# The first layer of a hybrid network: constants, norm and low-rank products inside one block

## What is computed

```python
h = layernorm(x)                       # 1024 rows of 256
q, k, v = (silu(conv4(h @ W, c)) for W, c in ((Wq, cq), (Wk, ck), (Wv, cv)))
w = l2norm(silu(conv4(h @ Ww, cv)))
g = log_sigmoid(h @ Wf1 @ Wf2)         # decay of each slot
beta = sigmoid(h @ Wb)                 # write strength of each head
o = gsa2_scan(q, k, v, w, g, beta)     # recurrence over 512 tokens
gate = h @ Wg1 @ Wg2 + bg2
x = x + (rms_norm(o) * norm_w * sigmoid(gate)) @ Wo
```

## Time and profile before

| | us |
|---|---|
| median of 3 runs | 2630.3 (2629.23 to 2631.29) |
| profiled execution, its own time | 2630.27 |
| its span, first to last instruction | 2628.5 |
| PE busy | 2331.3 (89%) |
| VectorE busy | 1678.3 (64%) |
| ScalarE busy | 1192.8 (45%) |
| Pool busy | 1100.5 (42%) |

### The profile page before, as it was taken

One profiled execution on the slowest core, in us unless ns is written; L12 is line 12 of the kernel. 1 busy time (PEld: TensorE's weight loads), 2 busy tenths in 40 slices (PEclk: granted clock), 3 DMA queues, 4 the chain that ended last, 5 costly groups with the idle time before them and its releaser, 6 DMA issues. The chain is left out here.

```text
span 2628.5 us, 49074 instructions
## 1 busy us (share of the span) xinstructions
PE 2331.3 (89%) x18400; PEld 1614.6 (61%) x18400; DVE 1678.3 (64%) x3286; ACT 1192.8 (45%) x2937; POOL 1100.5 (42%) x1264
## 2 busy tenths in 40 slices
PE   5888888888888889888858999999889989999999
PEld 3467754777547775477745666677533356666685
DVE  3857777577776777667726777752366557777613
ACT  3655465554554546545424555532115535555411
POOL 0367632676326763277634544430030025444300
PEclk9999999999999999999978999999889989999999
DMA  2100000000010000000004000000100030000000
GB/s 46 49 6 2 2 17 32 6 2 2 17 33 5 3 2 17 17 2 2 2 1 120 19 19 19 7 1 1 49 1 1 1 114 19 19 19 13 1 1 17
DMA packets 57625, 46.30 MB, mean 18 GB/s; under 512 B 11560, under 2 KB 50864, under 8 KB 57008
## 3 DMA queue, kind: packets, MB, share of 16 engines
q1 hardware_dynamic: 57392, 43.16, 5.6%
HBM read 42.10 MB, written 1.05 MB: 16 GB/s over the span
## 5 line engine op out<-in xcount | busy, mean ns | idle before, releaser
L1153 DVE SCALAR_TENSOR_TENSOR work<-four,taps,work 128x511 f32<-128x511 f32 (+2 forms) x384 | 284.7, 748 | 127.1 <-ACT work L849 117.5
L1761 POOL TENSOR_TENSOR rot<-q_plain,ropes 128x512 f32<-128x512 f32 x64 | 81.0, 1266 | 574.7 <-ACT q_plain L1792 574.7
L599 PE MATMUL four<-xT,wring 128*128 128x512 f32 x512 | 252.8, 621 | 6.6 <-DMA wring<-in_Wk_dram 4.8
L906 ACT ACTIVATE work<-four 128x512 f32<-128x512 f32 x216 | 129.0, 597 | 269.4 <-PE four L678 243.4
L729 PE MATMUL four<-work 128*128 128x128 f32 x1536 | 217.0, 286 | 0.0
L1805 ACT ACTIVATE pr<-four,nmaxf 128x512 f32<-128x512 f32 (+3 forms) x256 | 133.8, 525 | 171.4 <-DVE nmaxf L1643 171.4
L1643 DVE TENSOR_REDUCE nmaxf<-four 128x1 f32<-128x512 f32 (+3 forms) x256 | 125.7, 491 | 125.6 <-PE four L1486 120.8
L729 PEld LDWEIGHTS four<-work 128*128 128x128 f32 x1536 | 193.4, 196 | 3.9
L1484 PE MATMUL four<-rot,rot 128*128 128x512 f32 (+3 forms) x512 | 179.5, 446 | 5.5 <-DVE rot L1635 3.8
L1088 POOL TENSOR_TENSOR work<-work 128x256 f32<-128x256 f32 x184 | 145.6, 791 | 78.0 <-DVE work L1217 57.4
L1095 POOL TENSOR_TENSOR work<-work 128x256 f32<-128x256 f32 x184 | 141.7, 770 | 84.2 <-PE bank L763 74.6
(11 more groups left out here) (266 smaller groups left out, 5430.9 us busy)
## 6 DMA issues: line engine op xcount, KB each, us to landing
wqkv<-in_f_wq_dram SPq DMA_DIRECT2D x32, 128.0 KB, 2.3
wqkv<-in_f_wk_dram SPq DMA_DIRECT2D x32, 128.0 KB, 2.4
wqkv<-in_f_wv_dram SPq DMA_DIRECT2D x32, 128.0 KB, 2.4
wo<-in_f_wo_dram SPq DMA_DIRECT2D x2, 2048.0 KB, 11.7
we<-in_f_we_dram SPq DMA_DIRECT2D x4, 1024.0 KB
wring<-in_Wk_dram SPq DMA_DIRECT2D x4, 512.0 KB, 3.8
wring<-in_Ww_dram SPq DMA_DIRECT2D x4, 512.0 KB
wring<-in_Wv_dram SPq DMA_DIRECT2D x4, 512.0 KB, 3.9
```

Of the source, the lines that this page charges most:

```text
L599: last = nc.tensor.matmul(unit_bank(i)[:], wring[n % 2][:, c, h * P:(h + 1) * P], k.xT[:, c, b * T:(b + 1) * T], start=(c == 0), stop=(c = ...
L906: nc.scalar.activation(turned_keys(s, l), b3(key_bank), ACT.Copy).then_inc(key_kept, 1)
L1153: ins = nc.vector.scalar_tensor_tensor(out=cbuf[i % 4][:, n:], in0=unit_bank(i)[:, 0:T - n], scalar=taps[:, {"q": 0, "k": 1}.get(kind, 2), ...
```

## The change

The blocks for the loads of x, for the norm and for the constants are gone for this layer. All their steps stand in the layer's own block. SP issues at its start: x in two halves, eye, Wk, the three taps and norm_w, Wb, Ww, Wf1 and Wg1, Wf2, masks; each group of loads has a semaphore of its own (`x_in`, `taps_in`, `low_in`, `masks_in`). VectorE and ScalarE do the norm ahead of their first phase, in the same steps. PE turns x (`turn_x`) and then begins with phase 0. The write strengths are made tile by tile in phases 6 to 13 (`write_strengths`), the low-rank products in phases 20, 22, 24 and 26 (`low`), each behind what the phase held. ScalarE copies each product in the phase after it; `beta` is written in phase 14 as Tanh of half the argument, and Pool makes 0.5 * tanh + 0.5 of it. Wf1, Wg1 and Wb lie in another part of `work`, one that is not used until the slot loop.

```diff
+BETAS, LOWS = 6, (20, 22, 24, 26)
...
-        layer_norm(k, k.x, qT[:, 0].rearrange("p h t -> p (h t)").rearrange("p (t n) -> p t n", n=D), True)
...
-                pe.wait_ge(a_const, 8 * 16)
-                for m in range(2):
-                    for half in range(2):
...
+                x_rows = d["hidden_states"].rearrange("b (c p) n -> p (b c) n", p=P)
+                for half in range(2):
+                    sp.dma_start(k.x[:, 4 * half:4 * half + 4], x_rows[:, 4 * half:4 * half + 4]).then_inc(x_in, 16)
+                sp.dma_start(k.eye[:], d["c_eye"]).then_inc(x_in, 16)
                 load(KINDS[0], 0)
+                for n, name in enumerate(("cq", "ck", "cv")):
+                    sp.dma_start(taps[:, n], d[name].rearrange("(h p) j -> p h j", p=P)).then_inc(taps_in, 16)
...
+                    if g == 0 and i < 8 and i % HG == 0:
+                        pe.wait_ge(x_kept, DC * b + DC)
...
+                        if g == 0:
+                            pe.wait_ge(low_kept, 4)
...
+                def turn_x(half):
+                    pe.wait_ge(x_in, 48)
+                    pe.wait_ge(x_norm, 4 * half + 4)
+                    for c in range(DC):
+                        for t in range(4):
+                            last = nc.tensor.transpose(x_bank(half, c)[:, t * P:(t + 1) * P], xn[:, 4 * half + t, c * P:(c + 1) * P], k.eye[:])
+                        last.then_inc(x_turned, 1)
+
+                def write_strengths(t):
+                    if t == 0:
+                        pe.wait_ge(low_in, 48)
+                        pe.wait_ge(x_kept, 2 * DC)
+                    for c in range(DC):
+                        last = nc.tensor.matmul(result_bank[:, t * H:(t + 1) * H], k.xT[:, c, t * P:(t + 1) * P], wb[:, c, :],
+                                                start=(c == 0), stop=(c == DC - 1))
+                    if t == NT - 1:
+                        last.then_inc(beta_made, 1)
+
+                def low(n):
+                    m, half = n // 2, n % 2
+                    if n >= 2:
+                        pe.wait_ge(low_kept, n - 1)
+                    for c in range(DC):
+                        last = nc.tensor.matmul(low_bank(n)[:], wlow[:, m, c, :], k.xT[:, c, half * 512:half * 512 + 512],
+                                                start=(c == 0), stop=(c == DC - 1))
+                    last.then_inc(low_made, 1)
...
+                    if g == 0 and i in LOWS:
+                        low(LOWS.index(i))
+                    if g == 0 and BETAS <= i < BETAS + NT:
+                        write_strengths(i - BETAS)
+
+                for half in range(2):
+                    turn_x(half)
...
+                    if g == 0 and i - 1 in LOWS:
+                        n = LOWS.index(i - 1)
+                        act.wait_ge(low_made, n + 1)
...
+                    if g == 0 and i == BETAS + NT:
+                        act.wait_ge(beta_made, 1)
...
+                act.wait_ge(taps_in, 64)
...
+                    if g == 0:
+                        pool.wait_ge(beta_raw, 1)
+                        nc.gpsimd.tensor_scalar(beta[:], beta[:], 0.5, 0.5, ALU.mult, ALU.add).then_inc(beta_kept, 1)
+                        pool.wait_ge(beta_kept, 1)
...
+                dve.wait_ge(x_in, 48)
...
+                dve.wait_ge(taps_in, 64)
```

More of the change, by code:

```diff
@@ L353, in slot_attention @@
         work = sb("work", [P, WORK_WORDS])
-        a_const = sem("a_const")
-        low_made, low_kept = sem("low_made"), sem("low_kept")
-        layer_norm(k, k.x, qT[:, 0].rearrange("p h t -> p (h t)").rearrange("p (t n) -> p t n", n=D), True)
[L357 to L371, removed]
-                pe.wait_ge(a_const, 8 * 16)
-                for m in range(2):
-                    for half in range(2):
[L376 to L396, removed]
@@ L449, in slot_attention @@
         AH = {l: part(256).rearrange(hv, h=HG) for l in range(LOW, LEVELS)}
-        DG = part(512).rearrange(hv, h=HG)
-        PD = part(HG * QB).rearrange(hv, h=HG)
+        DG_PD = part(512 + HG * QB)
+        DG, PD = DG_PD[:, 0:512].rearrange(hv, h=HG), DG_PD[:, 512:].rearrange(hv, h=HG)
+        wlow = DG_PD[:, 0:2 * DC * P].rearrange("p (m c n) -> p m c n", m=2, c=DC)
+        wb = DG_PD[:, 2 * DC * P:2 * DC * P + DC * H].rearrange("p (c n) -> p c n", c=DC)
         tmp = part(256).rearrange(hv, h=HG)
@@ L477, in slot_attention @@
         gate_bank, y_bank, result_bank = k.bank[5], k.bank[4], k.bank[7]
+        low_bank = lambda n: k.bank[4 + n % 2]
+        x_bank = lambda half, c: k.bank[((1, 4), (5, 6))[half][c]]
         key_bank, turn_bank, qk_bank, out_bank = k.bank[0], k.bank[1], k.bank[6], k.bank[7]
@@ L1269, in pair @@
                         if l < LOW:
-                            dve.wait_ge(a_const, 8 * 16)
+                            dve.wait_ge(masks_in, 16)
                             dve.wait_ge(pair_made, order(PAIRS, g, s, l))
@@ L2167, in build, with _ @@
         rows = out.rearrange("b (c p) n -> p (b c) n", p=P)
[L2168 to L2175, removed]
+        if "A" not in layers:
+            with nc.Block() as block:
+                @block.sync
+                def _(sp):
+                    x_in = d["hidden_states"].rearrange("b (c p) n -> p (b c) n", p=P)
+                    sp.dma_start(k.x[:], x_in).then_inc(k.io_in, 16)
+                    sp.dma_start(k.eye[:], d["c_eye"]).then_inc(k.io_in, 16)
+                    sp.wait_ge(k.io_in, 32)
+        else:
             kept = len(k.sems)
```

33 lines of the change are left out of this document (32 added, 1 removed).

## The result

| | median us | runs | lowest to highest |
|---|---|---|---|
| before | 2630.66 | 4 | 2629.23 to 2631.29 |
| changed | 2606.32 | 4 | 2598.38 to 2609.29 |

The ratio is 0.9901 (95% interval 0.9887 to 0.9916): 24.3 us less, 26.6 forecast. The changed kernel's four runs spread over 10.9 us. The profiled execution of the changed kernel took 2609.29 us, its span 2607.41.

The account below looks back on a forecast made before the run. A start chain without overlap, then PE and VectorE both full in group 0's 32 units, were taken as the bound; -30.65 + 3.5 + 0.6 = -26.55 us gave 2603.7 us, within this case 2601.2 to 2606.4.

Parts of the forecast that it names:

- The start: Ahead of the first convolution: it begins at 19.3 us instead of 49.94, -30.65 us (from -31.3 to -29.65).
- Loads in a stack: Loads queued at the start: Wk behind x costs 0 to 0.2 us and lands at 7 to 9, well before needed.
- Rival (a): At the start: Wk and taps slow x's load, or taps land after 18.5; 2 to 4 us later; chance 0.14.
- Write strengths: Phases 6 to 13: 32 records at 0.108 us on PE without slack, paid in full, +3.5 us (3.4 to 4.3).
- Rival (d): First phase: narrow write-strength matmuls pull the clock to half; +37 us with units 6 to 20 so, 2641; chance 0.02.
- Low-rank products: Phases 20 to 26: first and third hidden, waits of 1.2 and 0.5 us at the others; sum +0.6 (-1.2 to +1.5).
- The credit of 1.16 us for the half clock that goes: Behind the first sum: PE no longer idles 2.07 us, so the half clock and VectorE's 1.16 us wait at 107.21 go.
- Rival (b): Phases 20 to 26: low-rank products not hidden, 6.9 us instead of 0.6, write strengths 4.3; 2610.8 us; chance 0.08.
- No table switch: Phase 14 on ScalarE: Tanh between two Silus needs no table load, 0 us.
- rival (c): Phase 14 on ScalarE: a table is switched twice, 2 x 1.28 us, +2.4, giving 2606.1 us; chance 0.01.
- The last convolution: End of the 32 units of group 0: near 100.7 us, which is 127.3 - 26.55.
- all that follows hangs on the end of those 32 units: Behind group 0: same instructions as before, so the later parts only shift with the units' end on VectorE; no term.

Follow-up runs that it names:

- e1_again: The changed kernel run again with no edit: median 2602.67 us, ratio 0.989 to the kernel before.
- e3_spread: Changed kernel with write strengths moved to phases 24 and 26, low-rank products 3 and 4 to phases 32 and 33: 2604.34 us, ratio 0.9895.
- e2_products_first: Changed kernel with write strengths and the four low-rank products put back between turning x and the first projection: 2614.83 us, ratio 0.9935.
- e6_halves: e3_spread with Pool's Tanh step after its power operation, and VectorE's statistics starting when x's first half has landed: 2597.93 us, ratio 0.9893.

## Why the prediction was right, and where it was not

Step by step, against the first trace of the changed kernel.

- **The start.** Forecast -30.65 for the first convolution; it moved from 49.94 to 19.60, -30.34. VectorE began 0.34 earlier, not 0.45, since eye landed 0.1 later than before; projection 0 took 18.80 - 15.65 = 3.15 us, where I took 2.9; from tap to convolution it was 0.80, not 0.72. In e1_again the records got short earlier, projection 0 took 1.99, below the 2.2 to 3.2 of the forecast, and the first convolution came at 18.19, before the forecast 18.6 to 20.3. How long PE stays at half clock varied in the kernel before too (first convolution at 49.94 and 48.16), which the single profile did not tell.
- **Loads in a stack.** Wk landed 5.9 us after its issue instead of 4.2, at 8.2, in the 7 to 9 of the forecast. The halves of x landed 4.1 and 5.0 after their issues and eye 4.8, so all was there at 6.57, against 6.43 before. Rival (a) did not come: by the Trainium skill ("DMA: Bandwidth & Descriptors", "Latency and other measured facts") memory latency grows from 0.2 us to 2 us at high load; Wk's 1.7 us more is of that size, though nothing here shows that the memory was the reason, and nobody waited for Wk.
- **Write strengths.** Forecast +3.5, measured 2.96: the pace was 2.60 us against 2.24, so 0.09 for a record and not 0.108. That PE had no slack in units 6 to 13 was right, and e3_spread shows it from the other side: at phases 24 and 26 they cost 0.15 at most. Rival (d) did not come: the granted clock was 1.00 from 20 to 100 us.
- **Low-rank products.** Forecast waits of 1.2 and 0.5, measured 1.01 and 0.43; the first and third hidden, as forecast. From the first sum to the last convolution's end it took 30.56 us instead of 30.18: +0.4 in all, forecast +0.6. The credit of 1.16 us for the half clock that goes was booked from one trace, as a fixed price of the gap; e2_products_first has the same gap of 2.07 us without it. Rival (b) did not come.
- **No table switch.** Tanh ran at 54.74 for 0.28 us and the next tap at 55.31, with no ACT_TABLE_LOAD between; the last one, at 21.16, stood ahead of the first Silu. The Trainium skill's list of sets ("ScalarE: Activation LUTs", "Table sets: the hidden batching unit") let rival (c) look possible; the trace decides against it. The order counts, though: in e2_products_first the Tanh at 23.52 ran on a table loaded at 16.37, and the first Silu needed another load of 1.28 us at 37.07. What Silu had loaded served the Tanh; what was loaded for the Tanh did not serve Silu.
- **The last convolution:** forecast near 100.7, measured 100.11.
- **The step that failed** is "all that follows hangs on the end of those 32 units", with nothing for what follows. The part behind took 2507.3 us in the first trace and 2499.1 and 2500.0 in two later ones; at the two places compared, the granted clock made 4.7 of the 8.2 us. In the profiled run 6 of the 27.2 us won at the last convolution were gone at the end. My range held the three medians (2606.3, 2602.7 and 2602.4), the first by 0.1 us, but single runs went from 2598.4 to 2609.3, beyond it on both sides, and the gains against the kernel before of the same series were 24.3, 27.5 and 23.2, the last below the 23.9 to 29.1 of the forecast. So the start and the units were right by their mechanism; that all three medians fell into 2601.2 to 2606.4 was partly luck. The four close times of the kernel before and its one profile hid a spread of its own of 19 us. The range should have carried some +-4 us for it.

## What to carry to other kernels

Of the 30 us ahead of the first convolution that went, 15.1 were waits of PE for loads that could have been issued at the start (10.26 and 4.82), and 14.1 were PE work that nobody needed yet (26.38 to 40.51). Ask of each wait at a program's start which instruction needs the data, and issue loads in the order of need. Work that is moved under another engine's cover costs its full time where its own engine is full too (3.0 us in phases 6 to 13, 0.15 at most in 24 and 26), so look for stretches where another engine has extra work, and look again at every in-order list that the moved step feeds: Pool's wait for the Tanh cost PE 3.0 us and took back the gain. Before a change of under 1% is read from two profiles, compare the stretch that it touches by itself, and profile the same kernel twice to know what the rest does.

## What the runs showed of the hardware that was not expected

- The times of one kernel on one core spread by up to 19 us of 2600 (19.1 for the kernel before in one series, 18.7 for e2_products_first, 5 to 11 for most others), with PE at half clock (1.2 of 2.4 GHz) at other places: the same 120 records in 11.78 us at a mean granted clock of 0.81, and in 8.74 at 1.00.
- The same idle time of PE, 2.07 us behind the first sum, was followed by a stretch at half clock in both traces of the kernel before and by none in e2_products_first. Between the last convolution and the slots the same work took 14.84 us in the changed kernel's first trace and 13.16 in e1_again.
- 16 matmuls of 16 columns (32 records) in a row at the start took 0.22 us a record (e2_products_first), the length of half clock, and the first seven wide records behind them 0.85; the same narrow records in groups of four between projections took 0.09, at a granted clock of 1.00.
- The clock column of a profile can read 1.00 at a program's start while the records have the length of half clock: 1.00 for 16.50 to 23.30 us in e2_products_first, at 0.22 us a narrow record. Check it against the length of the records.
- The first of two 512 KB halves of x could be used from 4.88 us on, and the second landed at 6.4 (e6_halves), where VectorE waited for both and eye until 6.57.
- A Tanh ran on the table that Silu had loaded, and a Silu did not run on the one loaded for Tanh (a load of 1.28 us at 37.07 in e2_products_first).
